# First MLP of a convolution-window and attention block: four of six first-layer blocks issued one stage earlier

## What is computed

```python
out = jnp.einsum('bqk,bkc->bqc', attn, v)          # 14x14 window attention, 12 heads of 16
out = out.reshape(bw, WS, WS, DIM) @ proj_w + proj_b
x = shortcut + out
h2 = layernorm(x, n2_w, n2_b)
mlp = gelu(h2 @ lin1_w + lin1_b) @ lin2_w + lin2_b  # 192 -> 768 -> 192
return x + mlp
```

## Time and profile before

| | |
|---|---|
| median of 3 executions | 864.72 us (862.1 to 865.1) |
| the profiled execution's own time | 865.97 us |
| its span, first to last instruction | 863.8 us |
| mean granted TensorE clock | 0.977 of 2.4 GHz |
| TensorE matmul busy | 806.0 us (93%) |
| VectorE, ScalarE, GpSimd busy | 550.2, 509.1, 205.8 us |
| the first MLP, from its first product to the next stage's | 315.6 to 381.1 us |

### The profile page before, as it was taken

One profiled execution on the slowest core, in us unless ns is written; L12 is line 12 of the kernel. 1 busy time (PEld: TensorE's weight loads), 2 busy tenths in 40 slices (PEclk: granted clock), 3 DMA queues, 4 the chain that ended last, 5 costly groups with the idle time before them and its releaser, 6 DMA issues.

```text
span 863.8 us, 15316 instructions
## 1 busy us (share of the span) xinstructions
PE 806.0 (93%) x5240; PEld 652.8 (76%) x5240; DVE 550.2 (64%) x1212; ACT 509.1 (59%) x1045; POOL 205.8 (24%) x273
## 2 busy tenths in 40 slices
PE   3899989989998989998998999999999999999997
PEld 2776766676686669887887678985999678985997
DVE  6978688696877864657663775457634775456542
ACT  5777578658767733345553755645644756555552
POOL 3050031023001025555600450026000450026000
PEclk9989999989999989999998999999999999999999
DMA  7010000001000022421100303210131003210110
GB/s 214 1 43 2 1 17 24 0 0 36 0 1 0 2 68 99 166 78 50 38 1 7 122 1 109 63 67 0 55 104 60 18 0 109 71 58 0 56 55 19
DMA packets 16168, 39.19 MB, mean 45 GB/s; under 512 B 5696, under 2 KB 11072, under 8 KB 13568
## 3 DMA queue, kind: packets, MB, share of 16 engines
q1 hardware_dynamic: 12960, 26.08, 9.2%
q0 software_dynamic: 3168, 12.59, 4.6%
HBM read 32.37 MB, written 6.29 MB: 45 GB/s over the span
## 4 chain that ended last, share of the span: by engine, by line
PE 75%; DVE 12%; ACT 7%; issue 4%; POOL 1%; DVEq 0%; DMA 0%; SPq 0%; ACTq 0%; POOLq 0%
PE ps L249 18%; PE ps L1714 8%; PE ps L1352 7%; PE ps L1623 6%; PE ps L1748 5%; PE ps L1270 4%; PE ps L1719 4%; PE ps L1250 4%; PE ps L1442 4%; DVE area L311 2%; ACT area L1164 2%; PE ps L1258 2%; PE ps L1223 1%; PE ps L1648 1%; DVE area L662 1%
## 5 line engine op out<-in xcount | busy, mean ns | idle before, releaser
L249 PE MATMUL ps<-xs,ws 128*128 128x512 f32 x460 | 122.6, 417 | 5.7 <-DVE xs L577 3.9
L249 PE MATMUL ps<-ws,wx 128*128 128x512 f32 x480 | 115.4, 396 | 1.5 <-DVE ws L918 1.5
L249 PEld LDWEIGHTS ps<-xs,ws 128*128 128x128 f32 x460 | 88.4, 198 | 26.1 <-issue 6.9
L249 PEld LDWEIGHTS ps<-ws,wx 128*128 128x128 f32 x480 | 89.3, 188 | 23.5 <-issue 4.4
L929 DVE TENSOR_TENSOR ws<-ps,rounded 128x512 fp32r<-128x512 f32 x80 | 55.0, 688 | 76.3 <-ACT ps L1194 76.2
L1048 ACT ACTIVATE area<-ps,nm 112x196 f32<-112x196 f32 (+1 forms) x240 | 85.5, 439 | 19.7 <-DVE nm L721 19.7
L1714 PE MATMUL ps<-rounded 128*128 128x384 f32 x320 | 97.1, 360 | 0.0
L463 POOL TENSOR_TENSOR area<-area,dstat 128x512 f32<-128x512 f32 x32 | 38.0, 1197 | 245.1 <-DVE dstat L872 245.1
L1193 ACT ACTIVATE rounded<-ps,bcol 128x512 fp32r<-128x512 f32 x80 | 56.8, 710 | 60.2 <-PE ps L249 60.2
L721 DVE TENSOR_REDUCE nm<-ps 112x4 f32<-112x784 f32 (+1 forms) x72 | 63.0, 874 | 32.1 <-PE ps L1250 27.0
L1719 PE MATMUL ps<-rounded,ws 128*128 128x192 f32 x320 | 72.8, 258 | 2.5 <-DVE ws L929 2.5
(11 more groups left out here) (200 smaller groups left out, 1585.5 us busy)
## 6 DMA issues: line engine op xcount, KB each, us to landing
rounded<-w_kept SPq DMA_DIRECT2D x16, 1152.0 KB, 5.2
stage<-in_wall POOLq DMA_DIRECT2D x42, 128.0 KB, 2.4
w_kept<-rounded POOLq DMA_DIRECT2D x4, 1152.0 KB, 5.2
xplain<-in_w2e POOLq DMA_DIRECT2D x4, 576.0 KB, 6.8
out<-xres SPq DMA_DIRECT2D x4, 384.0 KB, 2.6
xres<-in_x SPq DMA_DIRECT2D x1, 1152.0 KB, 7.9
area<-in_wall SPq DMA_DIRECT2D x2, 512.0 KB, 6.0
area<-in_w2a SPq DMA_DIRECT2D x1, 576.0 KB, 3.8
```

The source lines that it names most:

```text
L249: last = mm(out_, l, r, start=n == 0, stop=n == len(pairs) - 1)
```

## The change

TensorE's blocks of the first layer become a helper `wide(m)`. In the tail of the last attention pair, blocks 0 to 3 of pair 1 are issued at steps 18 to 21, behind the turning and ahead of the values. In the MLP loop, a pair's own part begins with blocks 4 and 5, and blocks 0 to 3 of the next pair stand at its end. ScalarE no longer waits for the last attention residual (`o_res`) before the first Gelu, but for the last scores (`a_s`), since `hT` overwrites the queries. TensorE's wait for `o_res` at the start of the MLP stays, as do the lists of VectorE, GpSimd and SP.

```diff
-            act.wait_ge(o_res, 1 + 2 * PAIRS)
+            act.wait_ge(a_s, 1 + PAIRS * UNITS)
...
+            def wide(m):
+
+                product(ps[:, m % 4, :], (CL1 + m * P, CL1 + m * P + P), xcols(0, N)).then_inc(b_h, 1)
...
+                    if not nxt and UNITS <= u:
+
+                        if u == UNITS:
+                            pe.wait_ge(ln_split, PAIRS + 1)
+                            pe.wait_ge(w_split, A_CHUNKS - QKV_CHUNKS)
+                        if u == UNITS + 2:
+                            pe.wait_ge(a_p, base + UNITS)
+                        wide(u - UNITS)
...
-            pe.wait_ge(w_split, A_CHUNKS - QKV_CHUNKS)
             pe.wait_ge(o_res, 1 + 2 * PAIRS)

             def body_b(it, nxt):

-                pe.wait_ge(ln_split, it + (PAIRS + 1))
-                for m in range(MC):
-
-                    pe.wait_ge(b_gelu, 1 + it * MC + max(0, m - 3))
-                    product(ps[:, m % 4, :], (CL1 + m * P, CL1 + m * P + P), xcols(0, N)).then_inc(b_h, 1)
+                for m in range(4, MC):
+
+                    pe.wait_ge(b_gelu, 1 + it * MC + m - 3)
+                    wide(m)
...
+                if nxt:
+
+                    pe.wait_ge(ln_split, it + (PAIRS + 2))
+                    for m in range(4):
+                        wide(m)
```

## The result

Over 12 executions the changed kernel has a median of 866.41 us (865.19 to 870.87), the one before 863.19 us (860.58 to 865.10). The ratio is 1.0048, with a 95% interval of 1.0033 to 1.0062: slower by 0.5%, some 4 us. A second measurement gave 1.0053 (1.0030 to 1.0077). The forecast was 868.6 us from a median of 864.72, a ratio of 1.0045.

A forecast was written before the change was run, and what follows sets the result against it. TensorE, busy 806.0 of 863.8 us, was taken as the bound, with VectorE's norm holding the turning after the change. Turning +1.5 and clock +2.4 make +3.9 us on the median 864.72: 868.6 us, range 865.0 to 871.3.

The forecast's parts named there:

- Four blocks in the tail: Last attention pair: turning of unit 16 to last reciprocal takes 8.36 us instead of 4.42; projection starts 3.9 us later.
- Projection: Projection of the last attention pair: -0.4 us on its 3.86 us, with bounds of -0.9 and +2.0 us.
- Norm strand: VectorE's norm of MLP pair 2, from the second attention residual to the last L555: unchanged at 7.53 us.
- forecast start of the turning: Turning of MLP pair 2's tokens: at 325.9 against 324.36, +1.5 us; +1.0 to +3.9 by the projection's bounds.
- Clock: Some 4.3 us of TensorE idle ahead of pair 2's turning slows the turning and second layer: +2.4 us.
- the room of 2.23 us: At the attention-MLP boundary TensorE's strand ended 2.23 us after the norm's; all the change could gain there.
- The earlier Gelu: ScalarE's Gelu of blocks 0 to 3, run during the attention tail, buy nothing, since nothing waited for them.
- Loop: MLP loop, pairs 2 to 4: TensorE's order unchanged and the norm still bounds; priced 0, period 16.1 us.
- Rival B: Slower beyond 0.5%: slow clock covers most of pair 1's second layer; +5.1 us, thus 869.8; chance 0.36.
- Rival A: TensorE, not the norm, sets pair 2's turning: -3.0 us, thus 861.7; chance 0.04.
- Rival C: TensorE's clock holds or returns within 1 us of work: +1.0 to +1.5 us left, 866.0; chance 0.14.
- rival D: Blocks wait in the attention tail, so the move has no effect: 0 beyond the 3.9 us; inside the forecast's 0.46.

The follow-up runs named there:

- ScalarE's wait: Changed kernel with ScalarE's first Gelu put back behind the last attention residual: 1.0007 on the kernel before, median 863.29 us.
- the filler: Changed kernel plus matmuls whose result nobody reads in TensorE's idle stretches at the attention-MLP boundary: 1.0002 on the kernel before, median 864.23 us.
- the held blocks: Two runs, changed kernel with blocks 4 and 5 held: until VectorE's statistics of the next pair, 1.0040; until GpSimd's first norm step, 1.0034.
- the run with everything: Changed kernel with pair 1's blocks in TensorE's own gaps and pair 2's norm ahead of the last residual: 0.9949 on before, 858.14 us.

## Why the prediction was right

The mechanism was the one that the runs show: the turning waits for the norm behind a later residual, and slow clock falls on the second layer. The forecast ratio of 1.0045 against 1.0048 is closer than the terms, and so far luck. In the profiles the stretch grew by 34.45 - 28.62 = 5.8 us and by 31.39 - 28.62 = 2.8 us, where the sum had 3.9, and before is one draw as well.

**Four blocks in the tail:** forecast 8.36 us from the turning of unit 16 to the last reciprocal, measured 8.72. The copy in pair 3 issues its third and fourth product back to back. In a row they hold TensorE for 2.52 us (237.59 to the values at 240.11); apart, each holds it for 1.36, and the values behind, cut in two, take some 0.15 us more. That the fourth block's place "changes the sum by nothing" was short by these 0.4 us.

**Projection:** forecast 3.46 us, 4.65 in the first profile, 2.93 in the second of the same kernel, and 2.90 to 2.92 in the four runs that changed only what surrounds it (ScalarE's wait, the filler, the held blocks). It was inside the bounds, but the first profile has it 0.8 us above before, where -0.4 was forecast: it is a matter of the execution.

**Norm strand:** forecast 7.53 us; 7.52 in the changed kernel, and 7.49 to 7.56 in every profile that left the norm behind the residual. The turning waited for L555 as forecast, and the loss went when the norm and the wait of blocks 4 and 5 were taken off the residual. The forecast start of the turning was 325.9, it came at 327.57: 0.2 us from an earlier stage, 0.4 from the tail, 1.2 from the projection.

**Clock:** forecast +2.4 us on the second layer; 11.69 - 8.84 = +2.85 in the first profile, 10.35 - 8.84 = +1.5 in the second of the same kernel. In the second profile the clock fell as was said: full clock up to blocks 4 and 5, 4.28 us idle, then slow. In the first it was at 0.50 since the projection, the ten matmuls took 4.63 us, and the idle time was 2.23, not the 3 to 5 forecast. The filler shows that the clock has a share, and at least 1.4 us of the stretch in both profiles. It does not show that the clock is the larger part of the 4 us. Of the room of 2.23 us that the prediction set against the delay, 1.69 us was itself slow clock. With hardly any slow clock on either side the order costs some 3 to 4 us, above the +1.5 of the sum; before, with its slow clock at this boundary, is the slower by a part of that.

**The earlier Gelu** were priced at nothing, "nothing waited for them". For the wait this was right, for the clock perhaps not: they let blocks 4 and 5 run at once, and so open the gap in front of the second layer. In the profiles that moved the slow stretch; in the averages it is not clear of chance.

**Loop:** forecast 0; 0.9992 (0.9974 to 1.0010), and a period unchanged to 0.03 us.

Rival B and the forecast share one mechanism, and the executions of the changed kernel spread over both (865.2 to 870.9). Rival A is excluded by the bracket of the turning. Rival C is excluded by the clock rows for the two profiled executions; the others have no rows. As for rival D, TensorE has no idle time ahead of any of the four products in the tail.

## What to carry to other kernels

Work that fills an idle stretch of one engine must go into that stretch itself: the same four blocks cost 4.3 us between the values, ahead of the instruction the chain waits for, and two of them cost 0.15 us behind it. Before taking work out from over a second strand, read how long that strand is, and at which clock the cover was measured: here it had 2.2 us to give, of which 1.7 were slow clock. And where TensorE must wait anyway, it matters on which side of the wait its last free work lies: in the profiles here, a gap in front of work with room cost nothing, and a gap in front of work on the path cost 1.5 us or more.

## What the runs showed of the hardware

The granted clock fell to 0.50 some 1 us into the projection in the first profile of the changed kernel, behind an idle time of 1.79 us with full work ahead of it, and held at 1.00 through the same idle time and the same projection in the second profile. In one measurement 12 executions of the same kernel ran from 865.6 us (mean clock 0.987) to 871.0 us (0.974). Of the 5.0 us between its two profiles 2.8 lie ahead of the turning of unit 16, far from the change. Between the filler run and the first profile of the changed kernel the clock was worth 4.5 us at one stage boundary.

VectorE's cast of 128x512 numbers took 2.46 us beside a GpSimd tensor_tensor of 2.62 us, and 0.43 us without it; in the run with the norm first and the blocks between the values the second cast took 2.84 us beside one of 2.69. The Trainium skill, SBUF — State Buffer, section Who interferes with whom, says of such a pair that the later one blocks fully rather than slows down. In both runs the GpSimd instruction started first, and the cast ended 0.3 us behind it (323.71 and 323.43 in the run with everything), which agrees.
